# Attention products of a decoder layer laid out as pairs of heads in 64-row halves of the array

## The reference

```python
q, k, v = split_heads(x @ Wq + bq), split_heads(x @ Wk + bk), split_heads(x @ Wv + bv)
att = where(tril, q @ k.T / sqrt(16), -inf)          # 1024 x 1024, per batch and head
x = layernorm(x + softmax(att) @ v @ Wo + bo)
x = layernorm(x + cross_attention(x, ctx, mask))     # 64 keys, 16 heads
x = layernorm(x + down(silu(gate(x)) * up(x)))       # 256 -> 1024 -> 256, weights ternary,
                                                     # activations rounded to 8 bits
```

## Time and profile before

| | |
|---|---|
| median of 3 executions | 921.69 us (919.38 to 922.36) |
| profiled execution, time | 925.3 us |
| profiled execution, span of the instructions | 923.5 us |
| mean granted TensorE clock | 0.989 of 2.4 GHz |
| PE (TensorE products) busy | 876.4 us, 95% |
| PEld (its weight loads) busy | 470.1 us, 51% |
| DVE busy | 726.4 us, 79% |
| ACT busy | 585.3 us, 63% |
| POOL busy | 353.7 us, 38% |
| chain that ended last | PE 84%, DVE 6%, ACT 3% |

### The profile page before, as it was taken

How to read it: one execution, slowest core, us unless ns; L and a number is a source line. 1 busy time by engine, 2 the same in 40 slices (tenths; PEclk the granted TensorE clock), 3 DMA queues, 4 the chain that set the end, 5 groups by cost and what they waited for, 6 DMA issues and landing times.

```text
span 923.5 us, 17928 instructions
## 1 busy us (share of the span) xinstructions
PE 876.4 (95%) x6314; PEld 470.1 (51%) x6314; DVE 726.4 (79%) x1584; ACT 585.3 (63%) x779; POOL 353.7 (38%) x521
## 2 busy tenths in 40 slices
PE   6798999899999999999999999999999999999875
PEld 3553545445565544645465454654656453555634
DVE  3788878767888788887988789877897789835688
ACT  2357866436765568645775568646586659864485
POOL 6312426442534254551434334553324221252224
PEclk9999999999999999999999999999999999999998
DMA  6831422111212111200022001111021000010001
GB/s 180 152 130 61 71 55 80 50 56 35 69 36 69 33 44 61 78 22 16 19 86 69 8 23 59 52 53 36 29 75 47 2 2 1 1 48 1 2 1 46
DMA packets 52965, 45.19 MB, mean 49 GB/s; under 512 B 12944, under 2 KB 51600, under 8 KB 52880
## 3 DMA queue, kind: packets, MB, share of 16 engines
q1 hardware_dynamic: 51024, 40.90, 14.9%
q0 software_dynamic: 1536, 3.15, 1.7%
q10 hardware_dynamic: 320, 0.00, 0.0%
HBM read 14.49 MB, written 4.19 MB: 20 GB/s over the span
## 4 chain that ended last, share of the span: by engine, by line
PE 84%; DVE 6%; ACT 3%; SPq 2%; DMA 2%; issue 2%; POOL 0%; ACTq 0%; POOLq 0%; DVEq 0%
PE ps L931 15%; PE ps L916 13%; PE ps L900 13%; PE ps L721 9%; PE ps L741 6%; PE ps L876 5%; PE ps L807 3%; PE ps L703 3%; PE ps L903 3%; PE ps L710 3%; PE ps L887 2%; DVE shift L1243 2%; PE ps L834 2%; PE ps L846 2%; PE ps L829 2%
## 5 line engine op out<-in xcount | busy, mean ns | idle before, releaser
L1243 DVE TENSOR_REDUCE shift<-ps 128x1 f32<-128x512 f32 (+3 forms) x608 | 371.2, 654 | 72.6 <-PE ps L903 43.1
L1030 ACT ACTIVATE probs<-ps 128x1024 f32<-128x1024 f32 (+3 forms) x384 | 299.9, 810 | 167.9 <-PE ps L916 166.2
L900 PE MATMUL ps<-k_stack,q_stack 96*128 96x512 bf16 (+3 forms) x768 | 211.0, 332 | 4.3 <-DMA q_stack<-part_sb 3.8
L916 PE MATMUL ps<-q_stack,k_stack 97*128 97x512 bf16 (+3 forms) x768 | 183.0, 328 | 5.1 <-DMA q_stack<-shiftT 2.9
L643 POOL TENSOR_SCALAR_AFFINE_SELECT probs<-probs 128x512 f32<-128x512 f32 x128 | 81.1, 635 | 247.8 <-ACT probs L1030 247.1
L931 PE MATMUL ps<-probs,v_aug 128*32 128x512 f32 (+3 forms) x1536 | 156.4, 496 | 1.7 <-POOL probs L643 1.3
L900 PEld LDWEIGHTS ps<-k_stack,q_stack 96*128 96x128 bf16 x768 | 74.0, 98 | 103.3 <-issue 32.3
L916 PEld LDWEIGHTS ps<-q_stack,k_stack 97*128 97x128 bf16 x768 | 64.6, 98 | 90.1 <-ACT probs L1030 33.9
L903 PE MATMUL ps<-causal,ident_h 128*128 128x128 bf16 x512 | 99.3, 222 | 0.0
L679 POOL TENSOR_TENSOR rstd<-veps,half_c 128x4 f32<-128x4 f32 (+1 forms) x27 | 25.5, 946 | 139.2 <-DVE veps L1202 139.2
L931 PEld LDWEIGHTS ps<-probs,v_aug 128*32 128x32 f32 x1536 | 33.9, 108 | 61.4 <-issue 47.5
(11 more groups left out here) (199 smaller groups left out, 1375.4 us busy)
## 6 DMA issues: line engine op xcount, KB each, us to landing
q_stack<-part_sb SPq DMA_DIRECT2D x192, 64.0 KB, 2.5
k_stack<-part_sb SPq DMA_DIRECT2D x144, 64.0 KB, 2.5
xt<-in_x SPq DMA_DIRECT2D x8, 512.0 KB, 3.9
out_x<-xt SPq DMA_DIRECT2D x7, 512.0 KB, 2.8
x_next<-in_x SPq DMA_DIRECT2D x6, 512.0 KB, 4.4
k_stack<-part_sb POOLq DMA_DIRECT2D x48, 64.0 KB, 3.3
q_stack<-shiftT SPq DMA_DIRECT2D x128, 1.0 KB, 1.7
y<-in_x SPq DMA_DIRECT2D x2, 512.0 KB, 4.8
```

Of the source, the lines that this page charges most:

```text
L900: mm = pe.matmul(ps[:, u.bank, j * w:(j + 1) * w], q_stack[0:KR, c, h, qb % TH * P:(qb % TH + 1) * P], k_stack[0:KR, h, k0:k0 + w], start= ...
L916: mm = pe.matmul(ps[:, u.bank + i, 0:BANK - off], k_stack[0:SH + 1, h, kb * P:(kb + 1) * P], q_stack[0:SH + 1, c, h, off:BANK], start=True ...
L1030: act.activation(probs[:, n % PROBS, 2 * pair:2 * pair + 2, 0:BANK - off], ps[:, u.bank:u.bank + 2, 0:BANK - off], ACT.Exp).then_inc(probs ...
L1243: dve.tensor_reduce(first[:, k0 // BANK, heads[0]:heads[-1] + 1, qb % TH], ps[:, u.bank, 0:len(heads) * w].rearrange("p (h w) -> p h w", w=w),
```

## The change

`q_stack` and `k_stack` get two parts. Part 0 holds four of the six pieces (`MAIN = 4`), part 1 the other two, the row with the maxima (or the ones), and zeros. In both, even heads of a group lie on partitions 0 to 63 and odd heads on 64 to 127. The maxima are computed from part 0 alone, as products over 64 rows for two heads, one in each half of the rows, into two neighbouring banks. The scores are the sum of a 64-row product of part 0 and one of part 1, again for two heads. The mask is added by products over 64 rows too, so two of them per head: 128 and 64 columns. The units of `m` take a pair of banks now, scores also the pairs from 5 and 6. DVE reduces two banks in one instruction. `kq` is taken out of PSUM by ACT. Constants grow, and part 1 of both stacks is zeroed at the start (`k_stack` by DVE, `q_stack` by POOL). `ORDER` is written anew.

```diff
+MAIN = 4
-SCORE_BANKS, SUM_BANK = [0, 2], 4
+SCORE_BANKS, SUM_BANK = [0, 2, 5, 6], 4
...
-    "r7r6r7r6rxr7r5r7rr6grr7r5w3r2gw6r1r0rm7gm6m5m3m2m1gm7m0m6m5m3w2m1w7w2fr6fm7m5m0fm3m1w6m2m7m6a0a2m5m7fcffffaf"
+    "r7r6r7xr6rr7r5w6r7rgw6r5rr7gr3r6r5r2rw1gw0r7gm2r6m0m2m5w7m0m2m5m0ffm2r7m5w1fm2a0m5a2ffam0r7ffa2m5om0a2w7ffaa"
...
-    KR = len(Q_PART) * D
-    SH = KR
+    HALF = P // 2
+    SH = len(Q_PART) - MAIN
...
-        n = BANK // (w - k0)
+        n = min(BANK // (w - k0), HG // 2)
         if c > 0:
-            max_units[c] += [(qb, 0, BANK, [h], False) for h in range(HG)]
-        max_units[c] += [(qb, k0, w - k0, list(range(h, min(h + n, HG))), True) for h in range(0, HG, n)]
+            max_units[c] += [(qb, 0, BANK, [p], False) for p in range(HG // 2)]
+        max_units[c] += [(qb, k0, w - k0, list(range(p, p + n)), True) for p in range(0, HG // 2, n)]
...
-        n = 2 if u.kind in ("scores", "score2", "pv2") else 1
+        n = 2 if u.kind in ("scores", "max", "score2", "pv2") else 1
...
-        q_stack, k_stack = sb("q_stack", [P, QC, H, BANK], BF16), sb("k_stack", [P, H, T], BF16)
+        q_stack, k_stack = sb("q_stack", [P, 2, QC, H // 2, BANK], BF16), sb("k_stack", [P, 2, H // 2, T], BF16)
...
             for j, i in enumerate((K_PART, Q_PART)[t]):
-                engine.dma_start(stack[j * D:(j + 1) * D],
-                                 pieces_sb[n % SLOTS][rows, i, :]).then_inc(moved, 16)
+                at, part = slice(j % MAIN, P, MAIN), j // MAIN
+                dst = (k_stack[at, part, heads, h * BANK:(h + 1) * BANK], q_stack[at, part, h, heads, :])[t]
+                engine.dma_start(dst, pieces_sb[n % SLOTS][rows, i, :]).then_inc(moved, 16)
...
+            made(pool.memset(pick_h[:], 0.0))
...
+            made(pool.memset(q_stack[:, 1, :, :, :].rearrange("p c h q -> p (c h q)").bitcast(F32), 0.0))
             pool.memset(v2[:], 1.0).then_inc(consts_ready, 1)
+            pool.wait_ge(keys_zeroed, 1)
...
-                for j, hl in enumerate(heads):
-                    h = g * HG + hl
-                    mm = pe.matmul(ps[:, u.bank, j * w:(j + 1) * w], q_stack[0:KR, c, h, qb % TH * P:(qb % TH + 1) * P],
-                                   k_stack[0:KR, h, k0:k0 + w], start=True, stop=not diag)
+                for j, p in enumerate(pairs):
+                    h, end = g * HG // 2 + p, (j + 1) * w
+                    for s, rows in enumerate(four):
+                        mm = pe.matmul(ps[:, u.bank + s, end - w:end], q_stack[rows, 0, c, h, qb % TH * P:(qb % TH + 1) * P],
+                                       k_stack[rows, 0, h, k0:k0 + w], start=True, stop=not diag)
                     if diag:
-                        mm = pe.matmul(ps[:, u.bank, (j + 1) * w - P:(j + 1) * w], ident_h[:], causal[:],
-                                       start=False, stop=True)
+                        for s, rows in enumerate(four):
+                            pe.matmul(ps[:, u.bank + s, end - P:end], pick_h[rows, HALF:P + HALF], causal[rows, :],
+                                      start=False, stop=False)
+                        for s, rows in enumerate(four):
+                            mm = pe.matmul(ps[:, u.bank + s, end - HALF:end], pick_h[rows, 0:P], causal[rows, 0:HALF],
+                                           start=False, stop=True)
...
-                for i in range(2):
-                    h = g * HG + 2 * pair + i
-                    mm = pe.matmul(ps[:, u.bank + i, 0:BANK - off], k_stack[0:SH + 1, h, kb * P:(kb + 1) * P],
-                                   q_stack[0:SH + 1, c, h, off:BANK], start=True, stop=True)
+                h = g * HG // 2 + pair
+                for part in range(2):
+                    for i, rows in enumerate(four):
+                        mm = pe.matmul(ps[:, u.bank + i, 0:BANK - off], k_stack[rows, part, h, kb * P:(kb + 1) * P],
+                                       q_stack[rows, part, c, h, off:BANK], start=(part == 0), stop=(part == 1))
...
+                elif kind == "kq":
...
+                    ins = act.activation(full[:, n % 2, :], ps[:, k, :], ACT.Identity, bias=bias[:, e:e + 1], scale=scale)
...
-                    ins = dve.tensor_scalar(full[:, n % 2, :], ps[:, k, :], scale, bias[:, e:e + 1], ALU.mult, ALU.add)
...
-                                  ps[:, u.bank, 0:len(heads) * w].rearrange("p (h w) -> p h w", w=w),
+                                  ps[:, u.bank:u.bank + 2, 0:len(pairs) * w].rearrange("p j (h w) -> p j h w", w=w),
...
+            dve.memset(k_stack[:, 1, :, :].rearrange("p h t -> p (h t)").bitcast(F32), 0.0).then_inc(keys_zeroed, 1)
```

More of the change, by code:

```diff
@@ L593, in _ @@
             made(pool.memset(ones_h[:], 1.0))
+            made(pool.memset(pick_h[:], 0.0))
             made(pool.memset(causal[:], 0.0))
-            made(pool.affine_select(out=causal[:], in_=causal[:], compare_op=ALU.is_ge, fill=NEG, base=0,
-                                    pattern=[[-1, P]], channel_multiplier=1))
+            for rows in four:
+                made(pool.affine_select(out=pick_h[rows], in_=pick_h[rows], compare_op=ALU.not_equal, fill=1.0, base=HALF,
+                                        pattern=[[-1, P + HALF]], channel_multiplier=1))
+                made(pool.affine_select(out=causal[rows], in_=causal[rows], compare_op=ALU.is_ge, fill=NEG, base=0,
+                                        pattern=[[-1, P]], channel_multiplier=1))
             made(pool.memset(off_pick[:], 0.0))
@@ L892, in max_unit @@
                 c, g, i = u.idx
-                qb, k0, w, heads, diag = max_units[c][i]
+                qb, k0, w, pairs, diag = max_units[c][i]
                 free(u)
+                if (u.b, i) == (0, 0):
+                    pe.wait_ge(consts_ready, 1)
                 if i == 0:
@@ L938, in _ @@
                     pe.wait_ge(consts_ready, 1)
-                    pe.wait_ge(ones_moved, 16)
                 if u.kind == "max":
@@ L965, in take @@
                     ins = act.activation(xT[:, d, h * BANK:(h + 1) * BANK], ps[:, k, :], ACT.Copy)
+                elif kind == "kq":
+                    n = u.idx
+                    t, e, h = pieces[n]
+                    if b == 0 and n == 0:
+                        act.wait_ge(kq_loaded[1], 16 * (NG + 1))
+                    if b == 0 and n == 1:
+                        act.wait_ge(bias_scaled, 1)
+                    if b * NP + n >= 2:
+                        act.wait_ge(low_ready, b * NP + n - 1)
+                    bias, scale = ((bk_c, 1.0), (bqs_c, SCALE))[t]
+                    ins = act.activation(full[:, n % 2, :], ps[:, k, :], ACT.Identity, bias=bias[:, e:e + 1], scale=scale)
                 elif kind in ("yT", "x1T", "y2T"):
@@ L1114, in take @@
                 dve.wait_ge(unit_ready, u.ready)
[L1115 to L1124 removed]
+                if kind == "v":
                     if b > 0:
```

117 lines of the change are left out of this document (54 added, 63 removed).

## The result

| | before | after |
|---|---|---|
| median of 4 executions, us | 921.99 | 908.02 (906.87 to 908.27) |
| profiled execution, time and span, us | 925.3, 923.5 | 908.27, 906.5 |
| ratio of the times, 95% interval | | 0.9852 (0.9832 to 0.9872) |
| DVE busy, ACT busy, us | 726.4, 585.3 | 692.4, 603.2 |

The change makes the kernel 14.0 us faster by the medians and 17.0 us by the two profiled executions. 903.3 was forecast.

A forecast was written before the change was run, and what follows sets the result against it. TensorE's stream of products was taken as the bound. Terms -61.4 - 7 + 1 + 44 + 4 + 1 = -18.4 us took the profiled 925.3 to 906.9 and the median 921.7 to 903.3 us; range 880 to 932.

The forecast's parts named there:

- The bound: Whole kernel, chiefly 200 to 850 us: TensorE's stream of products sets the time, busy 645.7 of 650 us.
- Maxima, -61.4: Products for the maxima on TensorE: 294,912 columns, 122.9 us, run as fully overlapping pairs of halves, 61.4 us off.
- case D: TensorE's half-height products: weight loads not hidden, about 0.1 us each, 166 us in all, 1069 us; chance 0.03.
- Mask, -7: Mask products on TensorE: 128 and then 64 columns per pair of heads, 22.5 us instead of 29.7, 7 off.
- Scores, +1: Score products on TensorE: two rounds of paired 64-row products, as many columns in time; 1 us more, ends 0 and 3.
- Changes of shape, +44: TensorE's written order: 802 changes between tile shapes instead of 401, at 0.11 us each, 44 us more; ends 36 and 62.
- case C: On TensorE, tile-shape changes cost 0.155 us and masks save nothing: 928 us, with one of the two about 921; chance 0.09.
- Sum on TensorE: TensorE's stream: -61.4 for maxima, -7 for masks, +1 for scores and +44 for tile-shape changes.
- Banks, +4: TensorE's loads waiting for banks that DVE and ACT free: 4 us more; ends -10 and +33.
- rival B: Waits for pairs of banks become the bound: 110 more, 0.3 us uncovered each, 33 us instead of 4, 932; chance 0.15.
- DVE and ACT: Busy times: DVE falls to about 660 us, ACT rises to 607; neither on the path from 200 to 850 us, worth nothing.
- Start, +1: Kernel start: POOL's grown constants end at 18 instead of 12.6 us; 1 us more, ends 0 and 5.

## Why the prediction was right

**The bound** was named rightly: TensorE's stream. Added columns cost 0.8 of their length, halving DVE's reductions brought 5 us, and moving the projections between DVE and ACT nothing that can be measured.

**Maxima, -61.4**: two halves run beside each other, 0.22 us for a pair of 512 columns. Right, and case D (loads that show between pairs) fell with the same rows. The rule of the Trainium skill ("TensorE: Matmul & The Clock Gate", "The mechanism") that a load overlaps only with products in other rows doesn't hold for these products: L911, L915, L918 and L934 follow each other in the same rows with 0.22, 0.06 and 0.03 us, the length of their columns.

**Mask, -7**: 0.06 and 0.03 as taken. Right.

**Scores, +1**: from one round of L934 with 512 columns to the next pass 0.216 us (median), from one L916 to the next 0.219 before, and the two halves start 0.003 us apart. So next to nothing, as taken.

**Changes of shape, +44** (0.11 each): 86 less 42 us, so 44 over the whole traces, and 0.110 us each as a mean. Right in size. Single rows show 0.10, and the kernel before with 64-row maxima 0.096 for its faster execution; by these the term would be 40. One reading behind it was wrong: the 0.31 us of the visit to L834 aren't two changes at 0.155. Its two rounds start 0.53 us apart (410.88 and 411.41), 0.10 over their stream, in one shape. That leaves 0.09 for the way in and 0.12 for the way out, so case C's price had no ground.

**Sum on TensorE**: the terms came to -23.4 us of TensorE's time; its busy time in the middle fell by 20.0. Most of the 3.4 us is the first 50 us, where TensorE isn't the bound; I had counted all of the columns at full value. In both traces 34 of the 768 products of the maxima (11,264 of 294,912 columns) and 32 of the 512 pieces of the mask stand there, whose saving of 2.8 us isn't in the middle, and so do 8 of the 401 new changes, 0.9 us. That makes -21.5 for the middle; 1.5 us stay open.

**Banks, +4**: idle time grew by 3 us, while the waits nearly doubled. The size was right and rival B's mechanism is there, but covered. B's price needed 110 more waits of 0.3 us uncovered; there were 66 more, and they left 3 us.

**DVE and ACT**: 692 and 603 us, forecast 660 (at most 690 by the prediction's sign) and 607. DVE's step was mis-sized: I took 43 us for 288 reductions less, from the 0.15 us per instruction in the durations; busy time fell by 23. Instructions overlap at their ends, so busy time per reduction is less than the duration (371.2 us for 608, with 654 ns mean, would be 397.6). Summed by duration, they fell by 41 us (397.4 to 356.2), as I had reckoned. It didn't touch the time.

**Start, +1**: the first maximum started 1.5 us earlier. The constants were hidden, as said.

**The number**: -18.4 was forecast and the profiled executions differ by 17.0: the columns took away 68 us by their count, the changes of shape gave back 44, and the places where TensorE ran dry another 7 (42 before, 49 now, over the stream). The medians differ by 14.0, because the profiled execution before stood 3.3 us over its median and the one after 0.25. The forecast had carried the whole sum to the median; 3 of the 4.7 us that it missed are this.

## What to carry to other kernels

Halving the rows of products so that two run beside each other is worth half their columns, but each entry and exit of another tile shape costs about 0.11 us here; count both from the written order before deciding, and keep small helpers such as a mask in the shape of their neighbours (33 us here). In a list that all engines walk, moving units by up to three or six places cost more than the changes of shape that it saved, in all three such lists, so count on that price before mending such a list by hand. When a mechanism's waits double, look at whether TensorE itself idles before calling them the bound.

## What the runs showed of the hardware

A product over 64 rows is a shape of its own even when it stands alone between products over 97 rows with the same 128 columns: 0.10 us in, 0.10 out (400.62 to 401.37 in the kernel before with 64-row maxima). Leaving a shape isn't the same for all: 0.118 us out of the value products' 32 columns, 0.096 into them (medians of both traces). In one shape, pairs of 64 columns follow at 0.03 us with two weight loads each, which is as short as any product here was asked to be; no floor of issue showed at twelve instructions of the array (six loads, six products) in 0.31 us. The rows of this are those of L911, L915 and L918 in the timeline after (409.39 to 409.70).
